# A hash-routed expert layer in sorted blocks of 128 slots instead of every expert for every token

## The reference

```python
x = _layernorm(x + _L0_attn_ref(...))      # linear attention, 16 heads
x = _layernorm(x + _L0_xattn_ref(...))     # hash-routed experts, the layer that is changed
x = _layernorm(x + _L0_ffn_ref(...))       # 8 experts, all of them weighted by a router
x = _layernorm(x + _L1_attn_ref(...))
x = _layernorm(x + _L1_xattn_ref(...))
x = _layernorm(x + _L1_ffn_ref(...))
```

```python
expert_ids = jnp.minimum(tid // tokens_per_expert, E - 1)
for e in range(E):
    g = jax.nn.silu(jnp.einsum('bsd,fd->bsf', hidden_states, Wg[e]))
    u = jnp.einsum('bsd,fd->bsf', hidden_states, Wu[e])
    y = jnp.einsum('bsf,df->bsd', g * u, Wd[e])
    out = jnp.where((expert_ids == e)[..., None], y, out)
```

## Time and profile before

| | |
|---|---|
| median of 3 runs | 430.35 us (426.91 to 431.69) |
| span of the profiled execution | 429.5 us |
| TensorE busy | 413.5 us, 96% |
| VectorE, ScalarE, POOL busy | 59%, 56%, 63% |
| mean granted clock of TensorE | 0.997 |
| bytes moved | 39.29 MB, mean 91 GB/s |

### The profile page before, as it was taken

The page is one execution under the profiler, slowest core; times in us unless marked ns, Lnnn a source line. Parts: engine busy times, 40 slices in busy tenths (PEclk is TensorE's granted clock), DMA queues, the critical chain, the costliest instruction groups (busy, mean ns, idle before and its releaser), DMA issues.

```text
span 429.5 us, 9350 instructions
## 1 busy us (share of the span) xinstructions
PE 413.5 (96%) x3645; PEld 361.4 (84%) x3645; DVE 255.2 (59%) x637; ACT 241.6 (56%) x423; POOL 270.6 (63%) x237
## 2 busy tenths in 40 slices
PE   8999999999999999899999999999699999999994
PEld 7888999988889888788888899798578989888983
DVE  4778657748536338966654588655455676343243
ACT  4848654764484775352734767573526757554543
POOL 1744454564798577674876548457647386877763
PEclk9999999999999999999999999999999999999998
DMA  8644000021233313042222103121523332565402
GB/s 256 195 149 145 3 2 0 2 76 50 73 91 123 103 53 124 24 127 96 79 86 76 38 0 111 51 88 63 167 74 96 118 103 78 151 165 151 141 33 98
DMA packets 19623, 39.29 MB, mean 91 GB/s; under 512 B 2763, under 2 KB 7371, under 8 KB 19580
## 3 DMA queue, kind: packets, MB, share of 16 engines
q1 hardware_dynamic: 19004, 38.17, 28.8%
q10 hardware_dynamic: 576, 0.53, 0.4%
HBM read 37.08 MB, written 1.08 MB: 89 GB/s over the span
## 4 chain that ended last, share of the span: by engine, by line
PE 75%; DVE 10%; issue 4%; ACT 4%; DMA 3%; SPq 2%; POOL 1%; POOLq 0%; DVEq 0%; ACTq 0%
PE bank L492 13%; PE bank L493 13%; PE bank L495 13%; PE bank L762 8%; PE bank L764 7%; PE bank L763 7%; PE bank L842 2%; DMA pk_raw<-w_attn_dram 2%; PE bank L781 2%; PE bank L830 1%; DVE q_buf L1584 1%; DMA brow<-cw_dram 1%; PE bank L515 1%; PE bank L812 1%; PE bank L813 1%
## 5 line engine op out<-in xcount | busy, mean ns | idle before, releaser
L1307 POOL TENSOR_TENSOR h_lo<-hraw,h_hi 128x512 fp32r<-128x512 f32 x76 | 98.1, 1294 | 77.3 <-ACT h_hi L1097 77.2
L492 PE MATMUL bank<-xT_hi,pk_hi 128*128 128x512 f32 x256 | 102.9, 402 | 1.1 <-DVE hraw L1625 1.1
L493 PE MATMUL bank<-xT_hi,pk_lo 128*128 128x512 f32 x256 | 101.0, 395 | 0.0
L1097 ACT ACTIVATE h_hi<-hraw 128x512 fp32r<-128x512 f32 x76 | 47.8, 629 | 72.3 <-DVE hraw L1625 70.3
L1625 DVE TENSOR_TENSOR hraw<-bank,sil 128x512 f32<-128x512 f32 x76 | 52.4, 689 | 54.6 <-ACT sil L1085 24.6
L495 PE MATMUL bank<-xT_lo,pk_hi 128*128 128x512 f32 x256 | 80.4, 395 | 0.0
L762 PE MATMUL bank<-pk_hi,h_hi 128*128 128x256 f32 x272 | 77.8, 286 | 0.2 <-issue 0.2
L764 PE MATMUL bank<-pk_hi,h_lo 128*128 128x256 f32 x272 | 76.9, 283 | 0.0
L763 PE MATMUL bank<-pk_lo,h_hi 128*128 128x256 f32 x272 | 76.8, 282 | 0.0
L1313 POOL TENSOR_TENSOR pk_lo<-pk_raw,pk_hi 128x512 fp32r<-128x512 f32 (+1 forms) x44 | 74.8, 1700 | 2.8 <-ACT pk_hi L1115 2.6
L492 PEld LDWEIGHTS bank<-xT_hi,pk_hi 128*128 128x128 f32 x256 | 48.2, 188 | 11.8 <-DVE hraw L1625 1.6
(11 more groups left out here) (256 smaller groups left out, 736.6 us busy)
## 6 DMA issues: line engine op xcount, KB each, us to landing
...
pk_raw<-pk_f_dram SPq DMA_DIRECT2D x16, 512.0 KB, 3.5
pk_raw<-pk_f_dram SPq DMA_DIRECT2D x16, 256.0 KB, 3.3
kv_buf<-pk_x_dram SPq DMA_DIRECT2D x4, 512.0 KB, 3.7
...
pk_raw<-pk_x_dram SPq DMA_DIRECT2D x4, 256.0 KB, 6.2
brow<-cw_dram SPq DMA_DIRECT2D x4, 256.0 KB, 3.4
cw_late<-cw_dram SPq DMA_DIRECT2D x4, 256.0 KB, 4.0
```

What stands on the lines that cost most here:

```text
L492: pe.matmul(o, w(kc)[0], x(kc)[0], start=kc == 0, stop=False)
L493: pe.matmul(o, w(kc)[1], x(kc)[0], start=False, stop=False)
L1097: A(h_hi[:, row, at * 512:(at + 1) * 512], hraw[:, s % 2, :], ACT.Copy).then_inc(sems["hid_hi"], 1)
L1307: pool.tensor_tensor(h_lo[:, row, q], hraw[:, s % 2, :], h_hi[:, row, q].bitcast(F32), ALU.subtract).then_inc(sems["hid_lo"], 1)
```

## The change

The hash-routed layer now computes only what a token needs. Each half's 512 tokens are sorted by expert into 7 blocks of 128 slots (`NB = 4 + 4 - 1`: as many as four tiles can need, when every expert's last block may be part empty). Each block belongs to one expert.

- *Placing* (`k` steps). VectorE makes the one-hot table of experts, TensorE counts with a triangular matrix how many tokens of the same expert stand ahead of each (`x0_rank`, 8 small products), and VectorE derives each token's slot (`slot_i`) and the place of each block's weights (`block_w`).
- *Sending* (`P`). After the norm, POOL scatters each tile's 128 rows by `slot_i` into a DRAM buffer `xs_dram` of 896 rows per half, which SP has cleared before. SP loads the 7 blocks of a half in one transfer of 896 KB (`L`).
- *Blocks* (`x<half>.<stage><block>`). Stage 0 transposes a block, stage 1 is the gate product (6 matmuls of 256 columns), with silu and multiply behind it, stage 2 transposes the hidden values, stage 3 is the down product. TensorE reads `block_w` into registers, 7 values ahead of each half's first gate, and takes the weights from that place.
- *Fetching* (`Y`, `Q`, `x*.4*`). ScalarE copies a block's result to SBUF, SP stores it in pairs of blocks (the seventh alone) to `ys_dram`, POOL gathers each token's row, and VectorE adds it to `x_tok` and takes the norm's statistics.

The dense units, their masked adds and the transposes `n0.2`, `n1.2` are gone, and the numbers of all later steps are 16 lower for `g`, `u`, `s`, `m`, `h`, `l` and 8 lower for `d` and `a` (`g16` is now `g0`).

```diff
+NB = HT + EX - 1
+U_F0, U_F1 = 0, 2 * E0
...
+b0.0 b0.1 k0 b0.2 b0.3 b1.0 b0.4 b0.5 b0.6 b0.7 b1.1 b0.8 b1.2 b0.9 b1.3 b1.4 b1.5 b1.6 b1.7 b1.8 b1.9 x0.00 x0.01
+x0.10 x0.02 x0.11 x0.03 x0.12 x0.20 x0.04 x0.13 x0.21 x0.30 x0.05 x0.14 x0.22 x0.31 x0.06 x0.15 x0.23 x0.32 x0.16
...
+        x_sent = (sm[:, :, :].rearrange("p t k -> p (t k)"), pT[:, :, :].rearrange("p a k -> p (a k)"))
+        y_sent = (kx[:, 1, :], kx[:, 0, :])
+        ones_m, tri_m = sil[:, 0, 0:P], sil[:, 0, P:2 * P]
+        tab = hraw[:, 0, :]
...
+            for h in range(2):
+                sp.dma_start(xs_dram[h][:, :].rearrange("(j p) d -> p j d", p=P),
+                             zero_r[:, 0:D].bitcast(F32).unsqueeze(1).to_broadcast([P, NB, D])
+                             ).then_inc(sems["x0_zero"], 16)
+            def x0_load(h):
+                if h:
+                    sp.wait_ge(sems["x0_t_ps"], 3)
+                sp.wait_ge(sems[f"x0_sent{h}"], 16 * HT)
+                rows = xs_dram[h][:, :].rearrange("(j p) d -> p j d", p=P)
+                to = x_sent[h][:, 0:NB * D].rearrange("p (j d) -> p j d", d=D)
+                sp.dma_start(to, rows).then_inc(sems["x0_in"], 16)
...
+                sp.wait_ge(sems["x0_y"], J + 1)
+                sp.dma_start(ys_dram[h][j0 * P:(j + 1) * P, :].rearrange("(j p) d -> p j d", p=P),
+                             y_sent[h][:, j0 * D:(j + 1) * D].rearrange("p (j d) -> p j d", d=D)
+                             ).then_inc(sems[f"x0_ys{h}"], 16)
...
+                pe.matmul(ranks, tri_m, per_tile, start=True, stop=False, skip_group_check=True)
+                for t in range(1, HT):
+                    pe.matmul(ranks[:, :, t:HT, :], ones_m, per_tile[:, :, 0:HT - t, :], start=False, stop=t == HT - 1,
+                              skip_group_check=True)
+                for t in range(HT):
+                    m = pe.matmul(counts, ones_m, per_tile[:, :, t, :], start=t == 0, stop=t == HT - 1,
+                                  skip_group_check=True)
+                m.then_inc(sems["rank_ps"], 1)
...
+                stage, J = i // 10, NB * h + i % 10
+                j = J % NB
+                if stage == 0:
+                    if j == 0:
+                        pe.wait_ge(sems["x0_in"], 16 * (h + 1))
+                    if J == 1:
+                        pe.wait_ge(sems["a0_res"], 4)
+                    for c in range(KC):
+                        a = j * D + c * P
+                        m = pe.transpose(x0_half(0, J)[:, c * P:(c + 1) * P],
+                                         x_sent[h][:, a:a + P], ident)
+                    m.then_inc(sems["x0_t_ps"], 1)
+                elif stage == 1:
+                    if j == 0:
+                        pe.wait_ge(sems["slots_ready"], 2)
+                        for k in range(J, J + NB):
+                            block_at[k] = pe.value_load(block_w[0:1, k:k + 1], min_val=0, max_val=(EX - 1) * W_X0)
+                    if J >= 2:
+                        pe.wait_ge(sems["x0_mul"], J - 1)
+                    pe.wait_ge(sems["x0_xh"], J + 1)
+                    o, at = x0_half(2, J), block_at[J]
+                    xh, xl = x0_cols(xT_hi, J), x0_cols(xT_lo, J)
+                    for c in range(KC):
+                        w = bass.ds(at + c * D, D)
+                        pe.matmul(o, xh[:, c, :], ew_hi[:, w], start=c == 0, stop=False)
+                        pe.matmul(o, xh[:, c, :], ew_lo[:, w], start=False, stop=False)
+                    pe.wait_ge(sems["x0_xl"], J + 1)
+                    for c in range(KC):
+                        m = pe.matmul(o, xl[:, c, :], ew_hi[:, bass.ds(at + c * D, D)], start=False, stop=c == KC - 1)
+                    m.then_inc(sems["x0_g_ps"], 1)
+                elif stage == 2:
+                    pe.wait_ge(sems["x0_mul"], J + 1)
+                    for c in range(KC):
+                        m = pe.transpose(x0_half(4, J)[:, c * P:(c + 1) * P],
+                                         hraw[:, J % 2, c * P:(c + 1) * P], ident)
+                    m.then_inc(sems["x0_v_ps"], 1)
...
+                    pe.wait_ge(sems["x0_hh"], J + 1)
+                    o, at = x0_half(6, J), block_at[J]
+                    hh, hl = h0_cols(h_hi, J), h0_cols(h_lo, J)
+                    for c in range(KC):
+                        w = bass.ds(at + c * D, D)
+                        pe.matmul(o, hh[:, c, :], ew_hi[:, w], start=c == 0, stop=False)
+                        pe.matmul(o, hh[:, c, :], ew_lo[:, w], start=False, stop=False)
...
+                    act.wait_ge(sems["x0_d_ps"], J + 1)
+                    j = J % NB
+                    A(y_sent[h][:, j * D:(j + 1) * D], x0_half(6, J), ACT.Copy).then_inc(sems["x0_y"], 1)
...
+            def x0_send(h):
+                pool.wait_ge(sems["x0_zero"], 32)
+                pool.wait_ge(sems["slots_ready"], 1)
+                for t in range(HT):
+                    T = HT * h + t
+                    pool.wait_ge(sems["ln_done"], 4 * nth(h) + t + 1)
+                    pool.indirect_dma_start(xs_dram[h][:, :], bass.IndirectOffsetOnAxis(ap=slot_i[:, T:T + 1], axis=0),
+                                            x_tok[:, T, :], None).then_inc(sems[f"x0_sent{h}"], 16)
+            def x0_fetch(h):
+                pool.wait_ge(sems[f"x0_ys{h}"], 16 * (NB // 2 + 1))
+                if h:
+                    pool.wait_ge(sems["x0_added"], HT)
+                for t in range(HT):
+                    T = HT * h + t
+                    pool.indirect_dma_start(o_tok[:, t, :], None, ys_dram[h][:, :],
+                                            bass.IndirectOffsetOnAxis(ap=slot_i[:, T:T + 1], axis=0)
+                                            ).then_inc(sems[f"x0_got{t // 2}"], 16)
...
+                    T = HT * h + t
+                    dve.wait_ge(sems[f"x0_got{t // 2}"], 32 * (h + 1))
+                    TT(x_tok[:, T, :], x_tok[:, T, :], o_tok[:, t, :], ALU.add).then_inc(sems["x0_added"], 1)
+                    dve.wait_ge(sems["x0_added"], T + 1)
+                    link(dve.bn_stats(stats[:, t, :], x_tok[:, T, :]))
```

347 lines of the change are left out of this document (230 added, 117 removed).

## The result

The changed kernel takes 447.88 us (median of 4 runs, 445.55 to 450.14) against 430.37 us: ratio 1.0416, 95% interval 1.036 to 1.0472. It is slower. The profiled execution has a span of 445.9 us against 429.5, so +16.4 us where I had worked out +9.4 and forecast 440 us.

The account below looks back on a forecast made before the run. TensorE, busy 96% of the span, was taken as the bound. Waiting of 29.8 us less 20.4 us of arithmetic gave +9.4 on 429.5, 438.9, forecast as 440 us; 8 in 10 from 425 to 457.

Parts of the forecast that it names:

- (a): Ahead of the first block: TensorE idles 5.1 us for the scatters, the DRAM round trip and the last projection's wait.
- (b): Reading the block table: 14 register reads ahead of the halves' first gates, 0.63 us each, 8.8 us (bounds 1.4 to 29).
- (c): Addresses from a register: 56 register steps between the blocks' gate matmuls, 0.04 us each, 2.2 us.
- (d): Clock: TensorE falls to half rate after three gaps of over 4 us; 3 us for all (bounds 0 and 9).
- rival 1: Block pipeline nearly free: reads 0.10 us each, registers nothing, clock stays; 427 us, faster or even; chance 0.27.
- the second rival: The clock falls at every gap, each restart 3 us, 9 in all: +15.4, 446 us; chance 0.2.
- (e): From the last block to the next layer: TensorE waits 6.4 us for half 0's aggregation and norm (bounds 5 and 9).
- (f): Start of the second layer: gate 2 waits for ScalarE, the first down product for POOL; 4.3 us (bounds 2 and 7).
- -20.4 of arithmetic: TensorE's net work: 47.0 us of dense layer and transposes leave, 26.6 us of blocks and rank table come.
- The 87%: Sign in the changed profile: TensorE's busy time falls and its share drops to some 87%.
- Rival 3: Half 0's gather is late, holding VectorE at its first add and TensorE with it: up to 4 us, 444; chance 0.08.

## Why the prediction was right, and where its sum was off

The sign, the range and the mechanism held: TensorE, full before, waits at the joints. The number, though, lies just inside the 433 to 448 us that I gave the forecast itself, and it does so because waits taken too long stand against a clock taken too cheap. Of the sum, +9.4 against +16.4, the terms came out so:

- **(a)** 5.1 us; measured 2.17 + 3.65 = 5.8. Two misses cancel. The first transposes came at 51.00 and not at 48.6: the first scatter began 1.5 us late (39.29 against 37.8), the four took 5.0 us (4.0), the write 1.5 (2.1), the load 5.3 (4.7). But the last projection ended late too, at 47.4 against 44.5, the half rate having its part in it.
- **(b)** 8.8 us; measured 3.97 + 4.25 = 8.2. That it fits is partly luck: the seven reads of the second group run from 69.7 to 74.8 us, 0.75 us from one to the next and not 0.63, and began beside matmuls that were still queued. The Trainium skill, DMA: Bandwidth & Descriptors, "Latency and other measured facts", gives a floor of about 0.6 us to such a load; the distance from read to read lies above it, the load alone under it, with a median of 0.31 us. What I missed is that 1.8 us of the first group is its true price there, and that the second cost 3 us more in clock.
- **(c)** 2.2 us; measured 0, by the run without registers: a round takes 1.87 us with them and without.
- **(d) is the step that failed.** I took 3 us for all restarts, of three gaps of over 4 us, and rival 1 leaned on "short gaps cost no clock in this trace". About 11.5 us were lost in half-rate matmuls, over the upper bound of 9. There were five stretches and not three, at 1.5 to 3.1 us each: one behind three gaps of 0.35 to 1.30 us, one behind a gap of 2.06 us. The run with matmuls on zeros shows what lay on the path, 5.9 us up to m0. So the second rival (446 us) came nearest the number, with waits that were too long and restarts that were too few. The price itself, 3 us, was read from the opening by the distance of its matmuls; the granted clock of the kernel before reads 1.00 there.
- **(e)** 6.4 us; measured 2.10 + 0.56, and 1.04 us in three gaps of the last rounds (0.43, 0.34, 0.27), in which VectorE does half 0's sums: 3.7. I had put the aggregation behind all of the last block; it comes at 92.75, beside it.
- **(f)** 4.3 us; measured 1.35 + 2.06 = 3.4.

The waits are thus 21.1 us and not the 26.8 of (a), (b), (c), (e) and (f); the clock is 8.5 more than taken. TensorE's busy time in the stretch falls by 5.1 us: -20.4 of arithmetic, some 10 of clock, 1.2 by which the opening moved, and about 4 us more. Two things can make them up, by an estimate from the timelines. The windows do not end at the same work: at 100 us the kernel before has done six gate and up steps of the next layer, at 116 us the changed one seven and 0.7 us of its first down product, together 2.1 us. And each of the 13 gaps adds the end of a matmul's record, 0.28 us against a distance of 0.12, at half rate 0.41 against 0.21, some 2.2 us. It is not the change from half to half: of the 3.94 us that pass there between two multiplies of the kernel with the reads first, one round is 1.87, and two more down products and six more transposes, which have to be done once in any order, are 12 x 0.12 + 6 x 0.10 = 2.04.

TensorE's share of the time is 92%. The 87% that I had given did not follow from my own sum, by which (413.5 - 20.4 + 3) / 438.9 is 90%.

Rival 1 (reads and registers nearly free, the clock staying) was wrong by its reads and its clock. Rival 3, the late gather: half 0's gather came late, issued at 80.44 since its last product stood behind the second group of reads, but its first sum at 87.41 had no wait. In the kernel with reads spread, half 1's blocks come sooner and TensorE has small gaps there (0.49, 0.70 us).
